# A wider first score pass in a causal cross-attention kernel: four array tiles for eight, one maximum for two

## What is computed

```python
def attention(Q, K, V):
    scores = jnp.einsum('bhqd,bhkd->bhqk', q, k) * scale
    scores = jnp.where(causal_mask, scores, jnp.finfo(scores.dtype).min)
    attn = jax.nn.softmax(scores, axis=-1)
    return jnp.einsum('bhqk,bhkd->bhqd', attn, v)

x = x + jnp.tanh(g_xattn[0]) * attention(_layernorm(x), ctx, ctx)
x = x + jnp.tanh(g_ffn[0]) * ffn(_layernorm(x), ...)   # top 4 of 16 blocks of 64 hidden units per token
```

## Time and profile before

| | |
|---|---|
| median of 3 runs | 695.56 us (695.04 to 695.76) |
| span of the profiled execution | 694.6 us |
| PE busy | 671.8 us, 97% |
| DVE, ACT, POOL busy | 519.7, 511.9, 564.2 us |
| mean granted clock of TensorE | 0.993 |

### The profile page before, as it was taken

The page is one execution under the profiler, slowest core; times in us unless marked ns, Lnnn a source line. Parts: engine busy times, 40 slices in busy tenths (PEclk is TensorE's granted clock), DMA queues, the critical chain, the costliest instruction groups (busy, mean ns, idle before and its releaser), DMA issues.

```text
span 694.6 us, 30557 instructions
## 1 busy us (share of the span) xinstructions
PE 671.8 (97%) x13072; PEld 623.5 (90%) x13072; DVE 519.7 (75%) x1429; ACT 511.9 (74%) x785; POOL 564.2 (81%) x778
## 2 busy tenths in 40 slices
PE   6779999999999999999999999999999999999998
PEld 5668899999999999999989999999999999999997
DVE  6788877877777787787787787778777777877752
ACT  3657787787787878778778777877877877786642
POOL 5687889889888888988988988898898888886642
PEclk9989999999999999999999999999999999999999
DMA  5322345444335354344444444533533544342010
GB/s 162 95 78 39 83 114 75 106 113 80 95 101 110 86 99 113 79 82 113 113 79 103 105 72 99 114 95 86 113 83 82 110 113 77 75 83 50 20 38 32
DMA packets 161814, 61.90 MB, mean 89 GB/s; under 512 B 135696, under 2 KB 161424, under 8 KB 161680
## 3 DMA queue, kind: packets, MB, share of 16 engines
q1 hardware_dynamic: 160848, 58.38, 37.7%
q10 hardware_dynamic: 832, 1.57, 0.8%
HBM read 19.03 MB, written 8.39 MB: 39 GB/s over the span
## 4 chain that ended last, share of the span: by engine, by line
PE 87%; DVE 4%; POOL 3%; SPq 2%; DMA 1%; issue 1%; ACT 1%; POOLq 0%; DVEq 0%
PE bank L411 10%; PE score_banks L332 10%; PE score_banks L302 8%; PE bank L413 8%; PE bank L412 8%; PE bank L436 8%; PE bank L435 8%; PE bank L434 8%; PE bank L345 8%; PE bank L359 4%; PE bank L370 3%; PE bank L381 1%; PE score_banks L315 1%; DMA qT<-qT 1%; PE bank L389 1%
## 5 line engine op out<-in xcount | busy, mean ns | idle before, releaser
L837 POOL TENSOR_TENSOR h_low<-hid,h_high 128x512 fp32r<-128x512 f32 x128 | 164.8, 1287 | 12.8 <-ACT hid L535 12.6
L709 DVE SCALAR_TENSOR_TENSOR hid<-bank,b_cols,used_all 128x256 f32<-128x256 f32 x248 | 108.2, 478 | 73.0 <-PE bank L413 66.9
L513 ACT ACTIVATE weights<-score_banks 128x1024 f32<-128x1024 f32 x128 | 124.3, 1023 | 40.3 <-PE score_banks L332 40.3
L411 PE MATMUL bank<-xT_high,w_high 128*128 128x256 f32 x496 | 150.7, 304 | 0.3 <-DVE hid L709 0.2
L830 POOL TENSOR_SCALAR_AFFINE_SELECT weights<-weights 128x1024 f32<-128x1024 f32 x128 | 138.3, 1105 | 8.6 <-ACT weights L513 8.2
L413 PE MATMUL bank<-xT_high,w_low 128*128 128x256 f32 x496 | 139.2, 281 | 0.0
L412 PE MATMUL bank<-xT_low,w_high 128*128 128x256 f32 x496 | 139.1, 280 | 0.0
L434 PE MATMUL bank<-w_high,h_high 128*128 128x256 f32 x488 | 137.3, 281 | 0.7 <-POOL h_low L837 0.7
L436 PE MATMUL bank<-w_high,h_low 128*128 128x256 f32 x488 | 138.0, 283 | 0.0
L435 PE MATMUL bank<-w_low,h_high 128*128 128x256 f32 x488 | 137.5, 282 | 0.0
L794 POOL TENSOR_SCALAR ve<-mv 128x1 f32<-128x1 f32 x128 | 34.6, 271 | 89.9 <-DVE mv L620 89.8
(11 more groups left out here) (102 smaller groups left out, 1508.4 us busy)
## 6 DMA issues: line engine op xcount, KB each, us to landing
x_in<-in_x SPq DMA_DIRECT2D x31, 256.0 KB, 3.3
out_y<-y_out SPq DMA_DIRECT2D x31, 256.0 KB, 2.4
c_in<-in_ctx SPq DMA_DIRECT2D x30, 256.0 KB
qT<-qT SPq DMA_DIRECT2D x128, 4.0 KB
w_stage<-in_w1T ACTq DMA_DIRECT2D x1, 1024.0 KB, 5.9
hid<-in_w2T SPq DMA_DIRECT2D x8, 128.0 KB, 2.7
kT_parts<-k_parts SPq DMA_TRANSPOSE x57, 2.8
qT_parts<-q_parts SPq DMA_TRANSPOSE x57, 2.7
```

What stands on the lines that cost most here:

```text
L411: pe.matmul(out=bank, lhsT=w1_high[:, k, c], rhs=high, start=k == 0, stop=False)
L513: act.activation(weights[:, b % 2, half * 2 * HB:(half + 1) * 2 * HB, :].rearrange("p h q -> p (h q)"), score_banks[:, 2 * half:2 * half + ...
L709: dve.scalar_tensor_tensor(hid[:, n % 4, j], hid_bank(n)[:, j * TOKS:(j + 1) * TOKS], b1_cols[:, c:c + 1], used_all[:, p % 2], ALU.add, AL ...
L837: pool.tensor_tensor(h_low[:, p % 2, chunks], hid[:, n % 4], h_high[:, p % 2, chunks].bitcast(F32), ALU.subtract).then_inc(h_low_made, 1)
```

## The change

The first pass takes all 128 queries and all 128 keys of a head in one product, on four array tiles of 32 rows by 128 columns, as the second pass does: 16 products for 32. The 16 masks are as many as before, each over 128 output partitions and 4 x 32 columns of one bank. The maxima come from one reduction over 2048 elements of each partition, and the maxima's row is copied by one transfer, so that `shifted_scores` waits for 16 where it waited for 32.

```diff
-    HALF = S // 2
-    WIDTH = HALF + S
@@ scores
-                for t in range(2):
-                    for late in (1, 0):
-                        for u in range(U):
-                            rows = slice(u * PAD, (u + 1) * PAD)
-                            for half in range(2):
-                                first = (2 * half + t) * S
-                                place_of = slice(half * HALF, (half + 1) * HALF)
-                                start = t * WIDTH + late * HALF
-                                pe.matmul(out=score_banks[place_of, u, start:start + (1 + late) * HALF],
-                                          lhsT=qT[rows, s, first + late * HALF:first + (1 + late) * HALF],
-                                          rhs=kT[rows, s, first:first + (1 + late) * HALF],
-                                          start=t == 0 and late == 1, stop=False, tile_position=(u * PAD, half * HALF))
+                for r in range(HB):
+                    cols = slice(r * S, (r + 1) * S)
+                    for u in range(U):
+                        rows = slice(u * PAD, (u + 1) * PAD)
+                        pe.matmul(out=score_banks[:, u, cols], lhsT=qT[rows, s, cols], rhs=kT[rows, s, cols],
+                                  start=r == 0, stop=False, tile_position=(u * PAD, 0))
-                for j in range(2):
+                for j in range(U):
                     for u in range(U):
                         rows = slice(u * PAD, (u + 1) * PAD)
-                        for half in range(2):
-                            per_head = score_banks[half * HALF:(half + 1) * HALF, u, 0:2 * WIDTH].rearrange(
-                                "p (t g k) -> p t g k", t=2, k=HALF)
-                            masked = pe.matmul(out=per_head[:, :, 0:3:2, j * PAD:(j + 1) * PAD],
-                                               lhsT=place[rows, j * P:j * P + HALF],
-                                               rhs=tri[rows].rearrange("p (t g) k -> p t g k", g=2),
-                                               start=False, stop=j == 1, tile_position=(u * PAD, half * HALF))
+                        per_head = score_banks[:, u].rearrange("p (r k) -> p r k", k=S)
+                        masked = pe.matmul(out=per_head[:, :, j * PAD:(j + 1) * PAD],
+                                           lhsT=place[rows, j * P:(j + 1) * P], rhs=tri[rows],
+                                           start=False, stop=j == U - 1, tile_position=(u * PAD, 0))
@@ shifted_scores
-                pe.wait_ge(max_landed[s], 2 * 16 * (b // TS + 1))
+                pe.wait_ge(max_landed[s], 16 * (b // TS + 1))
@@ row_maximum
-                ride = q_pad[:, carrier % QS, :, RIDE_COL].rearrange("p (t g u) -> p u t g", g=2, u=U)
-                found_in = score_banks[:, :, 0:2 * WIDTH].rearrange("p u (t k) -> p u t k", k=WIDTH)
-                dve.tensor_reduce(out=ride[:, :, :, 1], in_=found_in[:, :, :, HALF:WIDTH],
-                                  axis=AX_X, op=ALU.max, negate=True)
-                dve.tensor_reduce(out=ride[:, :, :, 0], in_=found_in[:, :, :, 0:HALF],
+                dve.tensor_reduce(out=q_pad[:, carrier % QS, :, RIDE_COL].rearrange("p (r u) -> p u r", u=U),
+                                  in_=score_banks[:].rearrange("p u (r k) -> p u r k", k=S),
                                   axis=AX_X, op=ALU.max, negate=True).then_inc(max_found, 1)
@@ max_row
-                for half in range(2):
-                    sync.dma_start(qT[MAX_COL::PAD, s, half * 2 * S:(half + 1) * 2 * S].rearrange("p (g q) -> p g q", q=HALF),
-                                   qT[RIDE_COL::PAD, ride % TS, :].rearrange("p (g f q) -> p f g q", f=2, q=HALF)[:, half]
-                                   ).then_inc(max_landed[s], 16)
+                sync.dma_start(qT[MAX_COL::PAD, s, :], qT[RIDE_COL::PAD, ride % TS, :]).then_inc(max_landed[s], 16)
```

## The result

| | before | changed |
|---|---|---|
| median | 695.66 us (695.04 to 696.48, 4 runs) | 705.27 us (702.15 to 705.86, 4 runs) |
| ratio to before | 1 | 1.0125, 95% interval 1.0105 to 1.0145 |
| span of the profiled execution | 694.6 us | 702.5 us |
| own time of the profiled execution | not on record | 704.87 us |

The changed kernel is 9.6 us slower by the medians and 8.7 by the ratio, where +10.2 was forecast (705.8). Its four executions are not alike: the span was 699.8 us at a mean granted clock of 0.998 and 703.3 at 0.987. Small differences between profiled executions therefore have to be read with the granted clock beside them.

A forecast was written before the change was run, and what follows sets the result against it. PE was taken as the bound in the steady part. PE +8.8, early tiles +1.3, maximum +1.2 and DMA -1.1 gave +10.2 us on the 694.6 us span, 704.8, so 705.8 us as time; range 700 to 713.

The forecast's parts named there:

- The bound: Whole kernel: PE busy 559.53 of 560.00 us from 80 to 640 us, so time added to PE there lengthens the end.
- The products: First pass on PE: 16 products on four tiles take 1.10 us, like L332, layout switch included.
- The masks: First pass on PE: 16 masks on four tiles, four turns of 128 columns at 0.06 us, 0.24 us in all.
- The rival of the load's pace: Masks on PE: loading 128 stationary columns sets their pace, 0.44 us a tile, time about 717 us; chance 0.07.
- The sum on PE: First pass per tile: 1.34 us for 1.18, +0.16 (+0.10 to +0.36); +8.8 us over 55 tiles at full clock.
- Streaming in full: Rival on the first pass: the two passes differ by all their streaming, 0.34 us more a tile, 716 us; chance 0.04.
- the prediction's aside: First-pass products: record count is part of the old pass's price, so 25% more columns cost PE little.
- Early tiles at the lower clock: Three first passes below 80 us, two at the lower clock (new pass there 2.57 us): together +1.3 us.
- The maximum: DVE reduction: 2.29 us for 1.90, hidden in steady tiles (1.24 us in hand), bare at three early places: +1.2 us.
- DMA: Maxima's row by one transfer: lands up to 0.57 us earlier at two waits of L332, -1.1 us.
- The fast rival: One early transfer removes all 10.2 us of L332's waits for the row, some 688 us; chance 0.04.
- From span to time: Whole kernel: runs' median lies 0.96 us above the profiled span, so span 704.8 becomes time 705.8.

The follow-up runs named there:

- two transfers: The changed kernel with the maxima's row copied by two transfers again, split in halves of the columns: 704.39 us, ratio 1.0114 to the kernel before.
- the short reduction: The changed kernel with its reduction over 104 of the 128 keys, 1664 elements a partition: 701.76 us, ratio 1.0079 to the kernel before.
- the longer maximum: The kernel before with one more VectorE reduction of 256 elements ahead of its two: 698.99 us, ratio 1.0058 to the kernel before.

## Why the prediction was right, point by point

*The bound.* PE busy 559.53 of 560 us was the right place to begin. The period of the steady tiles rose by 0.147 us, in tiles with the router (10.44 to 10.59) and without (9.98 to 10.13), and the pass by 0.146 us from first record to next layer.

*The products* were read off L332: 1.10 expected, 1.10 measured, switch included.

*The masks* were taken at 0.24 us by streaming and measured at 0.22. Their four turns start 0.056 us apart. The rival of the load's pace (0.44) is out. So is, for these masks, the floor of some 25 ns between matmuls that the Trainium skill gives ("TensorE: Matmul & The Clock Gate", Wait — 56ns, not 53.3ns?): 0.22 / 16 is 14 ns.

*The sum on PE.* +0.16 a tile forecast, +0.15 measured. 55 x 0.16 = 8.8 was forecast and 54 x 0.147 = 7.9 measured. The steady part shows 7.4, because the kernel before has one stall of 0.54 us in it, ahead of L332 at 362.8, which the profiled run of the changed kernel lacks. It lacks it with two transfers as well, so that is no merit of the single one. The records of the new products last 288 ns on the mean, where 270 was given as a sign.

*Streaming in full* was a rival at 716. The experiments place it: the extra columns alone cost 0.07 of 0.22 us in the old layout. They are a third more, and not the 25% of the prediction's aside. The rule of the Trainium skill on halved dimensions ("TensorEngine Tiling (Array Packing)", Theoretical Speedup) holds in direction. The eight-tile pass is the faster one, by 0.15 us, where streaming alone would give 0.34.

*Early tiles at the lower clock* were the weakest term: +1.3 us forecast. The pass that stood at 2.57 in the sum begins at 13.71 and its reduction at 15.84, 2.1 us later. The 2.09 of L332 was a pass wholly at 1.2 GHz, and this one was not. The granted clock was 0.50 in both stretches before and is 0.72 and 0.86 in them now. The lower level did not go away, it lies elsewhere. By stretch, changed kernel and kernel before, and the first pass of the third tile in the two chains:

```profile
16.00:24.00 8.00, 6.33 (x72) 5.36 (x75) 4.01 (x6) 5.20 (x9) 3.29 (x5) 0.50 0.45 131
16.00:24.00 8.00, 4.85 (x149) 3.89 (x148) 5.67 (x9) 5.56 (x9) 4.50 (x6) 1.00 0.47 137
...
22.50 2.01 PE score_banks L296 x32
...
20.89 1.02 PE score_banks L302 x45
```

That pass was not in the sum, and its products took 2.01 us where the wide ones take 1.10 at the full clock. The term thus rests on where the lower level falls in one execution, and no run here fixes that.

*The maximum* was sized well as an operation (2.29 forecast, 2.285 measured) and in its cover. Its price was not: three bare reductions, +1.2 us. With the reduction longer, the chain runs over seven of them ahead of 80 us. Some of them:

```profile
10.78 2.21 DVE q_pad L634
...
24.79 2.30 DVE q_pad L634
...
32.02 2.26 DVE q_pad L634
...
65.49 2.21 DVE q_pad L634
```

Seven times 0.40 would be 2.8 us, and the short reduction gave 3.2 to 3.5 back, or 1.6 by the estimate at equal clock; so the price lies above the forecast, by how much stays open. The step that failed is to count exposures in the chain of the kernel before: a chain lists who ended last, and an operation that grows joins the list where it was second.

*DMA* was -1.1 us in the sum, and no gain shows in the times. Where the chain had the wait at 73.11 it now has the reduction at 65.49, so the earlier row freed nobody that the reduction did not hold as well. The waits of L321 in the changed kernel say the same: 9.2 us for the reduction in six places, 0.2 us for the row. The fast rival, which wanted up to 10 us from the row, falls with it.

*The early part as a whole.* The terms for early tiles, maximum and DMA came to +1.4 us, and the tenth pass starts 0.6 us later. The single terms can't be added up to that: with the short reduction, whose DVE time is that of the kernel before, it starts 2.2 us earlier than before, wide passes and all. One transfer for two may show there once the reduction is out of its way, or the chain's other course; no run has the short reduction with two transfers.

*From span to time.* 0.96 us was added, the median of the runs less the profiled span; here the same difference is 2.77. In every execution whose span was kept, of either kernel, the time lies 1.7 to 2.4 us above its own span. The profiled execution of the kernel before was therefore one above the median, and that of the changed kernel lies 0.4 below its own. This term was 1.8 us short. The span was forecast at 704.8 and came at 702.5, so two errors of opposite sign left 705.8 beside 705.27. The agreement within 0.5 us is luck; the steady 7.9 for 8.8 us is not.

## What to carry to other kernels

Where an engine is busy without a gap, price a changed block by the block of the same form that the trace already holds: the second pass gave the new products' length to 0.01 us. In this kernel, packing narrow products on more array tiles paid less than their columns promise, and the wide form lost less than its extra columns suggest; that the records' own pace is the reason is likely, and not tested apart. A saving on another engine's queue may be worth nothing where the chain turns to a neighbour, and once the saturated engine is relieved, waits that carry an engine's name need not go when that engine gets faster.

## What the runs showed of the hardware that was not expected

VectorE's `xn` took 0.40 us in the kernel before. POOL was not idle then: it was ending `h_low`, and began its copy of the query parts for the last 0.2 us of it. Where the longer maximum pushes `xn` into this copy, it takes nearly twice as long. The timelines of the kernel before and of the one with the longer maximum:

```profile
340.31 1.28 POOL L837 TENSOR_TENSOR h_low<-hid,h_high 128x512 fp32r<-128x512 f32 x1
...
341.53 0.82 POOL L822 COPY q_parts<-q_pad 128x672 uint16<-128x672 uint16 x1
```

```profile
342.89 0.75 POOL L824 COPY q_parts<-q_pad 128x672 uint16<-128x672 uint16 x1
...
343.03 0.76 DVE L674 TENSOR_SCALAR xn<-x,mv,rstd 128x256 f32<-128x256 f32 x1
```

The steady tiles of four kernels order themselves so: with some 0.21 us of `xn` beside that copy it takes 0.40 us (kernel before), with 0.28 still 0.40 (short maximum), with 0.46 it takes 0.60 to 0.64 (changed kernel, 50 of 54 tiles), with 0.61 it takes 0.76 (longer maximum, 50 of 55). `xT_low` takes 0.42 us beside the copy of `v_pad` and 0.62 beside that of `k_parts`. In the changed kernel the means of xn and of xT_low rose from 540 and 499 ns to 627 and 637, which is 14 of DVE's 43 us, and the short maximum brought both back. So it is not POOL's being busy that counts, but which of its operations lies beside; the two beside which it is slower are copies of 16-bit elements. No run changed a copy alone, so that the copies are the cause is argued. The longer maximum eats 0.4 us of the time in hand and this as much again. So the 1.24 us that the prediction counted were spent twice as fast as it said, and still sufficed.

The narrow fp32 products cost some 16 ns a record (1.03 us for 64), the narrow bf16 products 8 ns (0.27 us for 32, from 407.19 to 407.46). Whether loading the stationary columns or the delivery of instructions sets this pace was not tested.
